# First stage of a layer kernel: two tiles per matmul for values and probabilities, the query bias inside its weights, inverse roots on ScalarE, another order at both ends

## The reference

```python
# stage 1: attention over a strided part of the context, 16 heads of width 8
x = x + xattn(layernorm(x), ctx, Wq, bq, Wk, bk, Wv, bv, Wo, bo, 16)
#   Q = hidden @ Wq.T + bq ; K, V likewise; each head sees 4 of the 77 rows:
#   idx = arange(16)[:, None] + 16 * arange(4)[None, :]
#   out = softmax(Q K^T * 8**-0.5) V ;  out @ Wo.T + bo
# and the routing of stage 2: gate = softmax(layernorm(x) @ Wg), idx = argmax,
#   loc = place of the token among those of its expert, dropped from 256 on
x = x + experts(layernorm(x), Wg, w1, w2)      # 16 experts, 128 -> 512 -> 128
# stage 3: causal attention of layernorm(x) over ctx
# stage 4: dense feed-forward plus 8 of 512 small experts per head
```

## Time and profile before

| | |
|---|---|
| median of 3 runs | 533.6 us (532.41 to 536.13) |
| the profiled execution | 534.3 us |
| its span, first to last instruction | 532.6 us |
| busy: PE, DVE, ACT, POOL | 415.9, 376.3, 348.5, 344.5 us |
| mean granted clock of TensorE | 0.885 |

### The profile page before, as it was taken

How to read it: one execution, slowest core, us unless ns; L and a number is a source line. 1 busy time by engine, 2 the same in 40 slices (tenths; PEclk the granted TensorE clock), 3 DMA queues, 4 the chain that set the end, 5 groups by cost and what they waited for, 6 DMA issues and landing times.

```text
span 532.6 us, 9386 instructions
## 1 busy us (share of the span) xinstructions
PE 415.9 (78%) x2528; PEld 344.0 (65%) x2528; DVE 376.3 (71%) x1628; ACT 348.5 (65%) x652; POOL 344.5 (65%) x251
## 2 busy tenths in 40 slices
PE   4968897819999639788667878889778787888956
PEld 3757786509999528676456657767566665776746
DVE  4457777402232147985989999999999999999970
ACT  2362654412222226986888889988898888998884
POOL 5226777740000175630789888898888988889882
PEclk9796889769999955865989998898999999889897
DMA  7981010023777111100000000000000000000000
GB/s 208 335 219 55 21 35 21 31 74 85 217 195 214 39 55 37 54 26 1 11 10 21 10 20 10 20 20 10 20 10 20 20 10 20 10 20 20 10 11 11
DMA packets 42418, 29.71 MB, mean 56 GB/s; under 512 B 4155, under 2 KB 38555, under 8 KB 42395
## 3 DMA queue, kind: packets, MB, share of 16 engines
q1 hardware_dynamic: 38539, 22.85, 14.9%
q0 software_dynamic: 2624, 6.30, 3.5%
q10 hardware_dynamic: 1232, 0.31, 0.3%
HBM read 18.95 MB, written 8.39 MB: 51 GB/s over the span
## 4 chain that ended last, share of the span: by engine, by line
DVE 22%; POOL 15%; ACT 12%; issue 5%; PE 4%; DVEq 1%; ACTq 0%; POOLq 0%
POOL arena_sb L484 15%; DVE picked_sb L1408 10%; ACT arena_sb L720 7%; ACT L720 4%; DVE bank L1370 2%; DVE first_sb L1367 2%; PE bank L1052 1%; DVE best_sb L1396 1%; DVE first_sb L1372 1%; DVE near_sb L1375 1%; DVE arena_sb L1421 1%; ACT xh_sb L510 1%; DVE pair_sb L1391 1%; ACT sc_sb L646 1%; PE bank L981 1%
## 5 line engine op out<-in xcount | busy, mean ns | idle before, releaser
L484 POOL TENSOR_TENSOR arena_sb<-arena_sb,picked_sb 128x2192 f32<-128x2192 f32 x32 | 154.4, 4846 | 25.6 <-DVE picked_sb L1408 25.6
L1408 DVE SCALAR_TENSOR_TENSOR picked_sb<-arena_sb,best_sb,bank 128x36 f32<-128x36 f32 (+1 forms) x256 | 107.7, 493 | 1.2
L1052 PE MATMUL bank<-ident_sb,arena_sb 128*128 128x128 f32 (+1 forms) x512 | 73.2, 305 | 34.6 <-DVE arena_sb L1421 30.9
L1052 PEld LDWEIGHTS bank<-ident_sb,arena_sb 128*128 128x128 f32 (+1 forms) x512 | 66.6, 169 | 39.8 <-issue 28.2
L476 POOL TENSOR_TENSOR arena_sb<-near_sb,sim_y_sb 128x1536 f32<-128x1536 f32 x32 | 87.7, 2759 | 1.3 <-DVE near_sb L1375 1.3
L720 ACT ACTIVATE arena_sb<-arena_sb,bsum_sb 128x548 f32<-128x548 f32 x128 | 85.6, 740 | 1.0 <-POOL arena_sb L484 0.8
L449 POOL DMA_INDIRECT picked_sb<-made,made_row_sb x32 | 30.7, 961 | 78.9 <-DMA made<-arena_sb 70.0
L714 ACT ACTIVATE arena_sb<-arena_sb 128x2192 f32<-128x2192 f32 x32 | 65.3, 2042 | 0.2
L1043 PE MATMUL bank<-w_down_t_sb,h_sb 128*128 128x128 f32 x256 | 34.8, 280 | 16.0 <-DVE x_all_sb L1427 15.3
L1043 PEld LDWEIGHTS bank<-w_down_t_sb,h_sb 128*128 128x128 f32 x256 | 31.1, 192 | 18.9 <-issue 18.9
L1031 PEld LDWEIGHTS bank<-xt_sb,w_up_t_sb 128*128 128x128 f32 x256 | 33.5, 192 | 14.8 <-issue 14.8
(11 more groups left out here) (176 smaller groups left out, 866.0 us busy)
## 6 DMA issues: line engine op xcount, KB each, us to landing
w_sb<-w SPq DMA_DIRECT2D x32, 256.0 KB, 3.4
x_all_sb<-x SPq DMA_DIRECT2D x8, 256.0 KB, 3.0
slots<-arena_sb POOLq DMA_DIRECT2D x4, 512.0 KB, 8.5
arena_sb<-slots SPq DMA_DIRECT2D x16, 128.0 KB, 3.1
made<-arena_sb SPq DMA_DIRECT2D x16, 128.0 KB, 1.9
xt_sb<-x_t_sb SPq DMA_DIRECT2D x32, 64.0 KB, 1.8
out<-x_all_sb SPq DMA_DIRECT2D x32, 64.0 KB, 1.5
ctx_t_sb<-ctx_t SPq DMA_DIRECT2D x8, 154.0 KB, 3.6
```

The costliest lines, as they stand in the source:

```text
L484: pool.tensor_tensor(pp[p][:, :, :], pp[p][:, :, :], picked[p][:, :, :], ALU.mult).then_inc(weighed, 1)
L1052: ins = pe.matmul(bank[4 * p][0:n, c * P:(c + 1) * P], pp[p][:, h, c * P:c * P + n], ident[:, :], is_transpose=True, start=h == 0, stop=h ...
L1408: ins = dve.scalar_tensor_tensor(out=picked[p][:, h, lo:hi], in0=vv[p][:, h, lo:hi], scalar=best[p][:, h, TOP - 1:TOP], in1=scores, op0=AL ...
```

## The change

**Two tiles per matmul.** A tile's `vm` and `attn` have 64 columns, so two tiles side by side have 128. `values` is now two matmuls with 128 output partitions in place of four with 64, `probabilities_t` two transposes in place of four. The even tiles of a half lie on partitions 0 to 63 of `uv` and `attn_t`, the odd ones on 64 to 127. `attention` still has four matmuls with 64 rows each, but first the two even tiles on the lower rows, then, after a wait on the new semaphore `o_even` for their end, the two odd ones on the upper rows. VectorE's addition into `uv` and ScalarE's copy into `attn_t` have 256 columns in place of 512.

**Query bias.** The matmul of the bias (L801) is gone. VectorE makes `wq_c` once, Wq plus a constant per row, (bq - the row's sum) / 128, and the bias of the first normalisation is one higher, so that each normalised token sums to 128 and the product gives back bq. `projected_keys` waits for `wq_c`.

**Roots.** ScalarE computes both inverse roots as Ln and then Exp with scale -0.5; one set of tables that holds both is loaded at the start. GpSimd keeps the two operations of each bias. `choice_shift` waits for the root on ScalarE, no longer for GpSimd's bias.

**Order.** At the start the roots of turn 0 are taken by halves, and on VectorE the second half's statistics come after the first keys. At the end the last `counts` is left out, the last `choice_shift` comes after the last `locations`, and in `rows` the operation that doesn't need the place stands first.

```diff
--- before.py
+++ after.py
...
-            def roots1(i):
-                pool.wait_ge(stat1_ready, 2 * i + 2)
+            def biases1(i):
+
+                pool.wait_ge(root1_ready, i + 2)
                 if i:
                     pool.wait_ge(xn_ready, 2 * i)
-                step(pool.tensor_scalar(ve[:, :], mv[:, :, 1], EPS, None, ALU.add))
-                step(pool.tensor_tensor(rstd[:, :], ve[:, :], minus_half[:, :], ALU.pow))
                 step(pool.tensor_tensor(nb[:, :], mv[:, :, 0], rstd[:, :], ALU.mult))
-                pool.tensor_scalar(nb[:, :], nb[:, :], -1.0, None, ALU.mult).then_inc(rstd1_ready, 1)
...
-            def roots2(i):
-                pool.wait_ge(stat2_ready, 2 * i + 2)
+                pool.tensor_scalar(nb[:, :], nb[:, :], -1.0, 1.0, ALU.mult, ALU.add).then_inc(rstd1_ready, 1)
+
+            def first_biases1(p):
+                tiles = slice(p * BT, p * BT + BT)
+                pool.wait_ge(root1_ready, p + 1)
+                step(pool.tensor_tensor(nb[:, tiles], mv[:, tiles, 0], rstd[:, tiles], ALU.mult))
+                pool.tensor_scalar(nb[:, tiles], nb[:, tiles], -1.0, 1.0, ALU.mult, ALU.add).then_inc(rstd1_ready, 1)
+
+            def biases2(i):
+                pool.wait_ge(root2_ready, i + 1)
                 if i:
                     pool.wait_ge(xh_ready, 2 * i)
-                step(pool.tensor_scalar(ve2[:, :], mv2[:, :, 1], EPS, None, ALU.add))
-                step(pool.tensor_tensor(rstd2[:, :], ve2[:, :], minus_half[:, :], ALU.pow))
                 step(pool.tensor_tensor(nb2[:, :], mv2[:, :, 0], rstd2[:, :], ALU.mult))
                 pool.tensor_scalar(nb2[:, :], nb2[:, :], -1.0, None, ALU.mult).then_inc(rstd2_ready, 1)
...
+                pool.wait_ge(oh_ready, i + 1)
+                step(pool.tensor_scalar(row_f[:, :], e_less[:, :], float(CAP), float(NE * CAP), ALU.mult, ALU.add))
                 pool.wait_ge(loc_ready, i + 1)
                 pool.tensor_scalar(valid[:, :], loc[:, :], float(CAP), None, ALU.is_lt)
                 step(pool.tensor_scalar(loc[:, :], loc[:, :], float(CAP - 1), None, ALU.min))
-                step(pool.tensor_scalar(row_f[:, :], e_less[:, :], float(CAP), float(NE * CAP), ALU.mult, ALU.add))
...
-            roots1(0)
+            first_biases1(0)
             step(pool.memset(zeros, 0.0))
+            first_biases1(1)
 
...
-            roots1(1)
+            biases1(1)
             for i in range(NI):
-                roots2(i)
-                counts(i)
+                biases2(i)
+                if i + 1 < NI:
+                    counts(i)
                 rows(i)
                 if i == 0:
                     pool.wait_ge(zeroed, 64)
                 scatters(i, 0)
                 if i + 2 < NI:
-                    roots1(i + 2)
+                    biases1(i + 2)
                 scatters(i, 1)
...
+            step = Steps(act, act_steps)
+
+            def root(dst, var, bias):
+
+                step(act.activation(dst, var, ACT.Ln, bias=bias[:, 0:1]))
+                return act.activation(dst, dst, ACT.Exp, scale=-0.5)
+
+            def roots1(i):
+                act.wait_ge(stat1_ready, 2 * i + 2)
+                if i > 1:
+                    act.wait_ge(rstd1_ready, i + 1)
+                root(rstd[:, :], mv[:, :, 1], eps1).then_inc(root1_ready, 1)
+
+            def first_roots1(p):
+                act.wait_ge(stat1_ready, p + 1)
+                tiles = slice(p * BT, p * BT + BT)
+                root(rstd[:, tiles], mv[:, tiles, 1], eps1).then_inc(root1_ready, 1)
+
+            def roots2(i):
+                act.wait_ge(stat2_ready, 2 * i + 2)
+                if i:
+                    act.wait_ge(rstd2_ready, i)
+                    act.wait_ge(lshift_ready, i)
+                root(rstd2[:, :], mv2[:, :, 1], eps1).then_inc(root2_ready, 1)
+
             def normalised(i, p):
-                act.wait_ge(rstd1_ready, i + 1)
+                act.wait_ge(rstd1_ready, i + 2 if i else p + 1)
...
-                copy(at_ready, attn_t[p][:, :, :], bank[4 + p][0:KA, :].rearrange("p (b t) -> p b t", b=BT))
+                copy(at_ready, attn_t[p][:, :, :], bank[4 + p][:, 0:BT // 2 * P].rearrange("p (b t) -> p b t", b=BT // 2))
...
                 probabilities_out(i, 0)
                 exps(i, 1)
+                if more:
+                    roots1(i + 1)
                 probabilities_out(i, 1)
...
                     tokens_out(i + 1, 0)
+                roots2(i)
+                if more:
                     keys_out(i + 1, 1)
                 slot_rows(i, 0)
                 if more:
...
+            act.preload_act_table_set("natural_log_exp_and_others")
+            act.wait_ge(consts, 1)
+            first_roots1(0)
             normalised(0, 0)
-            normalised(0, 1)
+            first_roots1(1)
             keys_out(0, 0)
             tokens_out(0, 0)
+            normalised(0, 1)
             keys_out(0, 1)
             tokens_out(0, 1)
...
             def projected_keys(i, p):
                 pe.wait_ge(km_ready, 2 * i + p + 1)
                 pe.wait_ge(vm_ready, 2 * i + p + 1)
-                pe.matmul(bank[p][:, 0:BT * KA], wq[:, :], km[p][:, :, :].rearrange("p b k -> p (b k)"),
+                pe.wait_ge(wq_ready, 1)
+                pe.matmul(bank[p][:, 0:BT * KA], wq_c[:, :], km[p][:, :, :].rearrange("p b k -> p (b k)"),
                           start=True, stop=True).then_inc(g_mm, 1)
 
             def values(i, p):
                 pe.wait_ge(g_ready, 2 * i + p + 1)
-                for t in range(BT):
-                    ins = pe.matmul(bank[p][0:KA, t * D:(t + 1) * D], vm[p][:, t, :], wo_t[:, :], start=True, stop=True)
+                for u in range(BT // 2):
+                    ins = pe.matmul(bank[p][:, u * D:(u + 1) * D], vm[p][:, 2 * u:2 * u + 2, :].rearrange("p b k -> p (b k)"),
+                                    wo_t[:, :], start=True, stop=True)
                 ins.then_inc(u_mm, 1)
 
             def tokens_t(i, p):
@@ -797,28 +835,32 @@
             def scores(i, p):
                 pe.wait_ge(xnt_ready, 2 * i + p + 1)
                 pe.wait_ge(g_ready, 2 * i + p + 1)
-                pe.wait_ge(wg_ready, 1)
-                pe.matmul(bank[2 + p][:, 0:BT * KA], bq_rows[:, :], km[p][:, :, :].rearrange("p b k -> p (b k)"),
-                          start=True, stop=False)
                 for t in range(BT):
                     ins = pe.matmul(bank[2 + p][:, t * KA:(t + 1) * KA], xn_t[p][:, t, :], gk[p][:, t, :],
-                                    start=False, stop=t == BT - 1)
...
-                for t in range(BT):
-                    ins = pe.transpose(bank[4 + p][0:KA, t * P:(t + 1) * P], attn[p][:, t, :], ident[:, :])
+                for u in range(BT // 2):
+                    ins = pe.transpose(bank[4 + p][:, u * P:(u + 1) * P],
+                                       attn[p][:, 2 * u:2 * u + 2, :].rearrange("p b k -> p (b k)"), ident[:, :])
...
-                for t in range(BT):
-                    ins = pe.matmul(bank[4 + p][:, t * D:(t + 1) * D], attn_t[p][:, t, :], uv[p][:, t, :], start=True, stop=True)
-                ins.then_inc(o_mm, 1)
+                for odd, done in ((0, o_even), (1, o_mm)):
+                    if odd:
+                        pe.wait_ge(o_even, 2 * i + p + 1)
+                    keys = slice(odd * KA, odd * KA + KA)
+                    for u in range(BT // 2):
+                        t = 2 * u + odd
+                        ins = pe.matmul(bank[4 + p][:, t * D:(t + 1) * D], attn_t[p][keys, u, :], uv[p][keys, u, :],
+                                        start=True, stop=True)
+                    ins.then_inc(done, 1)
...
-                dve.scalar_tensor_tensor(out=uv[p][:, :, :], in0=bo_rows[:, :].unsqueeze(1).broadcast_to([KA, BT, D]),
+                dve.scalar_tensor_tensor(out=uv[p][:, :, :], in0=bo_rows[:, :].unsqueeze(1).broadcast_to([P, BT // 2, D]),
                                          scalar=1.0 / HEADS_A,
-                                         in1=bank[p][0:KA, :].rearrange("p (b d) -> p b d", b=BT),
+                                         in1=bank[p][:, 0:BT // 2 * D].rearrange("p (b d) -> p b d", b=BT // 2),
                                          op0=ALU.mult, op1=ALU.add).then_inc(u_ready, 1)
...
             def choice_shift(i):
-                dve.wait_ge(rstd2_ready, i + 1)
+                dve.wait_ge(root2_ready, i + 1)
...
-                choice_shift(i)
+                if more:
+                    choice_shift(i)
...
             statistics1(0, 0)
-            statistics1(0, 1)
             dve.wait_ge(consts, 2)
             dve.wait_ge(wts_kv, 64)
             dve.wait_ge(wts_a, 16 * 5)
-            dve.tensor_copy(bq_rows[:, :], bq[:, :].broadcast_to([P, P])).then_inc(wg_ready, 1)
+
+            step(dve.tensor_reduce(wq_sum[:, :], wq[:, :], AXX, ALU.add))
```

(6 more changed lines are left out.)

23 lines of the change are left out of this document (11 added, 12 removed).

## The result

The changed kernel takes 531.3 us by the median of 11 runs (527.3 to 532.5), beside 534.1 us (531.4 to 536.1) for the kernel before: a ratio of 0.993, with a 95% interval of 0.991 to 0.996. I had forecast 523.4 us and a range of 519 to 529. It is faster by 0.7% and not by 1.9%. The profiled execution, 527.3 us with a span of 525.6, is one of the two shortest of the eleven, so its trace shows only part of what the median lacks.

The account below looks back on a forecast made before the run. No engine was taken as full: the first stage was a loop of waits, with GpSimd the next bound. Terms -3.4 - 4.2 + 0 - 2.6 = -10.2 us from 534.3 gave 524.1, or 523.4 us on the median's scale; range 519 to 529.

Parts of the forecast that it names:

- turn 1: First stage: shorter VectorE waits for scores, GpSimd's bias and `attention`, and a narrower `uv` addition, -3.4 us to 17.6.
- turn 2: First stage: shorter VectorE waits at the border, for exps, scores and `attention`, and a narrower addition, -4.2 us to 16.5.
- turn 3: First stage: keeps its length, as its waits on ScalarE and TensorE stay and no roots stood in its way; 0.
- tail: From the end of `onehot` to the second stage: root, counts and `row_f` leave GpSimd's path, less a wait; -2.6 us.
- The clock rival: Turns 1 and 2: TensorE granted only 0.70 of its clock, 5.2 us more, 528.6 us in all; chance 0.13.
- The wait on `o_even`: Between `attention`'s even and odd pairs: bounds nothing and 0.3 us, taken at 0.2 each; some six of eight count.
- -0.2 together: Turn 1, VectorE's two waits for `attention`, 1.1 us in all: the first loses its cause, the second gains the `o_even` wait.
- -0.8 of 1.2: Turn 2, VectorE's wait for `attention`: 0.8 of 1.2 us goes because TensorE starts on time.
- GpSimd's floor: Turn 2: with two root operations fewer per turn, a GpSimd that never waits still needs 16.5 us.
- turn 0 ends at 41.36: First stage's start: a queued DMA sets turn 0's end, so it stays at 41.4 us; no gain.
- ScalarE's roots hidden: Four new ScalarE operations per turn, 1.2 us, covered by its waits for transposes; cost nothing, or 1.2 us per turn uncovered.
- The stretch behind: Everything from the second stage's first transposes at 118.2 us on: 414.4 us, unchanged; over 1 us of change would refute.

Follow-up runs that it names:

- nopack: Changed kernel with the old unpacked `values`, transposes and `attention`, and no wait on `o_even`; 525.5 us, ratio 0.985.
- fullrows: Changed kernel, still packed, but `attention` over all 128 rows with zero-filled halves, an extra ScalarE copy and no wait; 523.8 us, ratio 0.981.
- inter: Changed kernel with the next block's keys and values between the even and the odd pair of `attention`; 544.1 us, ratio 1.021.
- waitonly: nopack with the wait on `o_even` between its two even and two odd tiles, all on the same 64 rows; 524.8 us, ratio 0.986.
- twobank: Changed kernel with `attention`'s odd tiles in another PSUM bank, alternating with the even ones, no wait, VectorE adding in two operations; 525.0 us, ratio 0.982.
- again: The changed kernel, unaltered, measured and profiled a second time; 531.1 us, ratio 0.994.
- fill: Changed kernel with unused bf16 matmuls in TensorE's gaps of turns 1 to 3 (80, 40 and 36); 524.2 us, ratio 0.981.
- ballast2: Changed kernel with each pair of `values` matmuls and probability transposes issued twice, first into unread columns; 524.5 us, ratio 0.981.
- fullwait: fullrows with the wait on `o_even` between even and odd tiles; 538.7 us where the kernel before takes 544.7, ratio 0.989.
- interbal: inter with each pair of `values` and of transposes issued twice; 539.1 us where the kernel before takes 544.7, ratio 0.990.

## Why the prediction was wrong

Span by span in the first profile, measured against forecast: turn 1 -2.2 (-3.4), turn 2 -4.2 (-4.2), turn 3 +3.2 (0), tail -2.5 (-2.6), the rest -1.3 (0), together -7.0 us (-10.2).

- **Turn 3: "its waits on ScalarE and TensorE stay ... 0" is the step that failed.** It lost 3.2 us, all of it behind the start of its second `attention` and at the lower level: 2.1 us for that block and 1.2 for the work behind it. As a gain, 0 was right (nopack 14.75, fullrows 14.55 us); but the turn had the full clock to lose.
- **The clock rival** named the mechanism and put it in the wrong place: I asked it only of turns 1 and 2, priced it at 5.2 us there and gave it 0.13. Its need, busy time times clock, was overstated, as it said itself: it took 14.3 us of work for turn 1, and the same product is 17.45 x 0.73 = 12.7 us in the changed kernel. And it expected a clock that falls behind gaps, while inter stayed at 0.50 with TensorE busy 24.34 of 24.50 us.
- **The wait on `o_even`**, taken at 0.2 us of 0 to 0.3, costs 1.41 - 1.08 = 0.33 us at the full level and 2.43 - 2.01 = 0.42 at the lower one (changed kernel less nopack), both above my upper bound. Still the size is small, eight times 0.1 to 0.2 us more than I took; in waitonly, where the clock mostly holds, it costs nothing that the runs can tell (0.986 beside 0.985, either to 0.005). With the packing it goes with a loss of 1%, and no term or rival had that. The Trainium skill's page "TensorEngine Tiling (Array Packing)", section "Gotcha 1: PSUM Pressure", says that different row tiles can't access one PSUM bank simultaneously and write to different banks. I had looked only at the rule on changing modes. twobank follows this one, with 0.65 us for the block and a ratio of 0.982 instead of 0.993; no run here lets two row tiles write to one bank at a time.
- **`attention`, "-0.2 together" in turn 1 and "-0.8 of 1.2" in turn 2**: the waits were to be 0.9 and 0.4 us and are 2.5 and 1.4. In turn 2 GpSimd's floor hides it; in turn 1 it is most likely where the missing 1.2 us are (twobank, which doesn't have this wait, takes 16.7 us there).
- **Right**: turn 0 ends at 41.36 (in the other profiles of such chips between 39.9 and 42.5, behind a wait of 1.2 to 7.5 us for the same data); no wait before `choice_shift`; GpSimd's floor of 16.5 us a turn, which eight kernels meet in turn 2 at 16.4 to 16.6; ScalarE's roots hidden; the tail to 0.1 us. The stretch behind moved by 1.3 us, more than the 1 us that I had called a refutation; over the kernels on that kind of chip it varies from 413.0 to 416.5, so the bound was too narrow.
- **The median.** I put the median 0.7 us below the profiled execution. For the changed kernel it is 4.0 us above. So of the 7.9 us between forecast and median the profiled execution has 3.2 and the difference between executions 4.7. The 3.2 are turn 3; that the 1.2 us of turn 1 don't show in the sum is luck, since the rest was 1.3 us shorter. That these are more time at the lower level, as in turn 2 of again, is likely and not shown.

The sum of -10.2 us was the right size for the change without the loss: twobank and fullrows reach 0.982 and 0.981 of 534.3, -9.7 and -10.3 us. For twobank that is partly luck: its turn 1 is 0.9 us shorter than forecast (16.7 for 17.6) and its turn 3 is 1.2 us longer than before. The best medians beside 534.7 us for the kernel before are 523.8 (fullrows), 524.2 (fill), 524.5 (ballast2) and, beside the same, 525.0 (twobank); these can't be told apart. twobank is the version I would keep, since it does no useless work and has the narrowest spread (524.9 to 525.2).

What stays open: which property of TensorE's work the level answers to. Added work kept it up in turn 3 (ballast2 0.88, fill 0.82), twobank only put its fall off (0.78), fullrows without a wait had 0.75, and busy time doesn't order the kernels. Whether the wait or the order in pairs counts, where the split by rows matters (fullwait) and why turn 1 of nopack ran low are open too.

## What to carry to other kernels

When a change takes work or adds a wait on TensorE, read the granted clock of every stretch, above all of those that the change doesn't mean to touch and that run at the full level now: that level is something to lose. A wait of an engine for itself between two halves of a block is cheap at the full level; at the lower one the whole block gets long, and it counts if another engine waits for it. Here it was better to write the halves to different banks than to order them. Compare two kernels from the same piece of work on, not at the same distance from a start. And profile twice: one trace of a kernel whose clock varies may be its best run.

## What the runs showed of the hardware

- Matmuls on rows 0 to 63 and on rows 64 to 127, alternating and into different PSUM banks, take 0.65 us for eight passes (twobank) instead of 1.08 on the same rows (nopack), both at the full level: they overlap.
- TensorE was busy for 99% of two turns (inter) and stayed at the lower level all the while; with added work in the same order, on another chip, it was at 0.85 and 0.91 (interbal).
- A wait of TensorE for its own matmuls in the middle of such a block costs 0.33 us at the full level (1.08 to 1.41 us) and 0.42 us at the lower one (2.01 to 2.43 us), nopack against the changed kernel.
